# Reordering the filling of a one-core Hyena and gated-MLP pipeline, with a one-sum inverse transform in three of sixteen halves

## The chip, the cores and the metric

One core of one Trainium2 chip runs the whole kernel in one launch. The metric is device microseconds of that core.

## The reference

The input x is 8 sequences of 512 positions by 512 channels. Two layers follow each other, each with a residual and a layer norm behind it:

```python
x = layernorm(x + attn(x)); x = layernorm(x + ffn(x))
# attn (a Hyena operator):
u = x @ in_proj_w.T + in_proj_b                  # 3 * 512 columns
uc = causal_conv1d_3taps(u, short_w) + short_b   # per channel
x0, x1, v = split(uc)
k = filter_network(sin, sin, sin) * decay        # 512 channels by 512 positions
v = irfft(rfft(v * x1, n=1024) * rfft(k, n=1024) / 1024)[..., :512] + (v * x1) * filter_bias
y = (v * x0) @ out_proj_w.T + out_proj_b
# ffn: int codes below 64, zero point 128, one scale for each row
y = (silu(x @ Wg.T) * (x @ Wu.T)) @ Wd.T         # 1408 hidden columns
```

## The kernel before, in words

**Tiling.** TensorE works in blocks of 128. A sequence has 4 position blocks and its channels are split into two *halves* of 256, so there are 16 halves. The MLP works on *pairs* of position blocks (256 positions); there are 16 pairs too. fp32 operands are split into a high and a low part and multiplied with three terms (`three`, L825 on).

**The pipeline.** `program()` writes one list of steps, and every engine walks the same list, taking the kinds it has a branch for. The list runs over n = 0 to 19 and eleven beats each. In iteration n: half n is projected (`ip`), convolved with three taps (`conv`), multiplied (`v1`: v*x1) and transposed (`tv`, `vsplit`); half n-1 gets its four block spectra (`fw`, two in beat 0, one in beats 3 and 6), the ten products spectrum x filter (`mul` on VectorE, two parts each, and `acc` on GpSimd, which adds them from a ring of four `tmp` slots into `acc`), the split of each finished block (`psplit`: ScalarE high part, GpSimd low part) and the inverse transform (`iv`), followed by the multiplication with X0 (`y`) and its split (`z`); pair n-2 gets its output projection (`op`), residual (`resid`, `ln1`) and LN1 (`stat`, `var`, `norm`); pair n-3 is transposed (`x2t`, `x2split`) and goes through the MLP (`gu`, `silu`, `hmul`, `hhi`, `hlo`, `dn`), one of eleven hidden blocks in each beat; pair n-4 is scaled (`ln2`), added (`x2add`), normalized and stored. So n = 0 to 2 are the *filling*, with no MLP, and n = 17 to 19 the *draining*.

**Products of a block.** Block i of a half is the sum over j <= i of spectrum j times filter i-j; `PAIRS_OF_BEAT` puts (0,0) in beat 0, (0,1) and (0,2) in beat 1, and so on to (3,3) in beat 8. `LIGHT` are the halves 0, 1 and 15. There the additions of block 3 are VectorE's *own* (L745 to L750), from `x2` slots or, for half 15, from `cv`; GpSimd skips them (L605).

**The inverse.** For each of two channel groups and two parts, `acc_hi` times the high and low inverse matrix side by side (256 columns), and `acc_lo` times the high one (128 columns): 8 matmuls, and a bank with two sums. `y` on VectorE takes three operations: low sum x X0, high sum x X0, their addition.

**Banks.** `bank` is a ring of two PSUM banks for ip, tv, iv, op, xt and x2t; until the MLP begins the two `gate_up` banks widen it to four. `free_bank` waits for the reading of the use before. The spectra have two banks of their own; a spectrum waits for the last product of the spectrum two before it.

**The network.** Three layers: a matmul (`net`, TensorE, L849), six operations on VectorE (same step name, L672 to L682), a sine on ScalarE (`sin`, L489); then `kmm` (L855) makes the filter from the last sine, and `spec` (L864, L866) its eight spectra, evicted by ScalarE (L493). The weights come as 18 floats stages (`stage`: ScalarE high part, GpSimd low part) and 35 integer code tiles (`code`: ScalarE; the down weights are saved to memory again by SP), through a few slots.

**The sequence of DMAs** is SP's: it walks the same list (`code`, `xload`, `resid`, `wdload`, `store`) and waits in order.

Lines that the prediction names: L741 product, L747, L749 and L750 own additions, L611, L617, L618 additions on GpSimd, L622 low part of a block, L639 bias into the residual rows, L648 rstd, L697 low part of x, L760 to L764 y, L778 scaling of `down`, L643 its addition, L558 normalization, L831 to L833 the three terms, L923 and L924 inverse, L945 transposition of x2, L962 and L963 gate and up, L973 and L974 down.

Of the kernel before, what the change touches and what calls it, by code (L numbers as in the profile page):

```python
# [177 lines left out]
def program():  # L178
    steps = [("xt", 0, 0), ("xt", 0, 1), ("xsplit", 0, 0), ("xsplit", 0, 1), ("stage", 0), ("stage", 1), ("xt", 0, 2),
             ("xt", 0, 3), ("xsplit", 0, 2), ("xsplit", 0, 3), ("net", 0), ("bias", )]  # L180
# [11 lines left out]
def build(nc, x, win, wout, wg, wu, wd, fwd, shifted, inv, decay, z_pos, w0, w1, w2, w3, net_cols, fbias,  # L192
          conv_w, conv_cols, gate_cols, up_cols, down_row, out_row, identity, out):
    ctx = ExitStack()
    with ctx:
# [271 lines left out]
        def _(act):  # L467
# [13 lines left out]
            for kind, *at in steps:  # L481
# [51 lines left out]
                elif kind == "psplit":  # L533
                    n, i = at
                    last = ("mul", n, i, i, 1)
                    if last in own:
                        act.wait_ge(own_added, own[last] + 1)
                    else:
                        act.wait_ge(temp_added, temp[last] + 1)
# [498 lines left out]
```

## Time and profile before

| | us |
|---|---|
| median of 3 runs | 1102.07 (1100.32 to 1104.34) |
| profiled execution | 1102.69, of which span 1100.9 |
| TensorE busy | 1036.5 (94%), weight loads 837.8 (76%) |
| VectorE, ScalarE, GpSimd busy | 803.1 (73%), 466.2 (42%), 625.9 (57%) |
| mean granted clock of TensorE | 0.970 |

The share of the span is an average over the stages: TensorE is at 90% or more in all slices from about 150 to 960 us of the span and at 70 to 90% before. The chain that ended last is 70% TensorE, 15% VectorE, 5% ScalarE, 4% GpSimd. In the rows below a time at the start of a line is microseconds from the start of the span; brackets give the idle time of the engine before the instruction and what ended it.

### The profile page before, as it was taken

How to read it: one execution, taken by the hardware profiler on the slowest of the kernel's cores; microseconds unless marked ns; L12 is line 12 of the kernel's file. 1: busy time of each engine (PE TensorE's matmuls, PEld its weight loads, DVE VectorE, ACT ScalarE, POOL GpSimd, SP SyncE). 2: the span in 40 equal slices, each digit the busy share in tenths (PEclk: the TensorE clock that was granted, in tenths of full speed). 3: DMA queues.
4: the chain of work that ended last, by engine and by line, in shares of the span. 5: the costliest groups of instructions: out<-in, count | busy, mean ns of one | idle time of the engine just before them, and what ended most of it. 6: DMA issues, size and time to landing. Idle time of an engine off the chain costs nothing.

```text
span 1100.9 us, 18043 instructions
## 1 busy us (share of the span) xinstructions
PE 1036.5 (94%) x6378; PEld 837.8 (76%) x6378; DVE 803.1 (73%) x1470; ACT 466.2 (42%) x995; POOL 625.9 (57%) x662
## 2 busy tenths in 40 slices
PE   7887869999999999999999999999999999979996
PEld 4465658888888888788888888888888888867774
DVE  5667777786877778786777778787777878777443
ACT  4554343444434444443444344443445344424242
POOL 4554636475674756576674766576574667572211
PEclk9897879999999999999999999999999999989998
DMA  7543311212123212212122211312121212222232
GB/s 226 169 150 120 101 58 58 82 45 88 48 77 95 79 59 67 97 49 86 49 78 87 87 52 65 99 56 80 55 78 49 87 49 63 72 58 77 87 94 79
DMA packets 51639, 89.53 MB, mean 81 GB/s; under 512 B 6298, under 2 KB 11034, under 8 KB 51550
## 3 DMA queue, kind: packets, MB, share of 16 engines
q1 hardware_dynamic: 50786, 88.12, 25.7%
q8 instruction: 51, 0.84, 0.3%
q10 hardware_dynamic: 764, 0.27, 0.1%
q14 instruction: 38, 0.31, 0.1%
HBM read 77.09 MB, written 11.27 MB: 80 GB/s over the span
## 4 chain that ended last, share of the span: by engine, by line
PE 70%; DVE 15%; issue 5%; ACT 5%; POOL 4%; DMA 1%; ACTq 1%; POOLq 0%; DVEq 0%
PE gate_up L962 10%; PE gate_up L963 10%; PE bank L831 9%; PE bank L833 8%; PE bank L832 8%; PE down L973 6%; PE down L974 6%; PE bank L923 2%; DVE hid_lo L821 2%; PE bank L945 2%; DVE tmp L741 1%; PE spectrum L831 1%; PE spectrum L833 1%; DVE hid L815 1%; PE spectrum L832 1%
## 5 line engine op out<-in xcount | busy, mean ns | idle before, releaser
L580 ACT ACTIVATE hid<-gate_up,gate_scale 128x256 f32<-128x256 f32 x176 | 83.0, 472 | 223.0 <-PE gate_up L963 221.8
L962 PE MATMUL gate_up<-x2T_hi,wg_sb 128*128 128x256 f16 x704 | 165.9, 276 | 0.0
L963 PE MATMUL gate_up<-x2T_lo,wg_sb 128*128 128x256 f16 x704 | 164.0, 273 | 0.0
L962 PE MATMUL gate_up<-x2T_hi,wu_sb 128*128 128x256 f16 x704 | 163.9, 273 | 0.0
L963 PE MATMUL gate_up<-x2T_lo,wu_sb 128*128 128x256 f16 x704 | 163.8, 273 | 0.0
L617 POOL TENSOR_TENSOR acc<-acc,tmp 128x256 f32<-128x256 f32 x148 | 114.9, 776 | 81.4 <-DVE tmp L741 72.0
L741 DVE TENSOR_TENSOR tmp<-spectrum,filt 128x512 f32<-128x512 f32 x235 | 159.5, 681 | 0.0
L973 PE MATMUL down<-wd_sb,hid_hi 128*128 128x512 f32 x352 | 148.3, 421 | 11.7 <-DVE tmp L778 7.2
L831 PE MATMUL bank<-xT_hi,win_hi 128*128 128x512 f32 x360 | 150.2, 417 | 1.2 <-POOL win_lo L598 0.6
L833 PE MATMUL bank<-xT_hi,win_lo 128*128 128x512 f32 x360 | 144.5, 401 | 0.0
L832 PE MATMUL bank<-xT_lo,win_hi 128*128 128x512 f32 x360 | 144.1, 400 | 0.0
L815 DVE SCALAR_TENSOR_TENSOR hid<-gate_up,up_scale,hid 128x256 f32<-128x256 f32 x176 | 84.2, 479 | 78.6 <-ACT hid L580 78.5
L974 PE MATMUL down<-wd_sb,hid_lo 128*128 128x512 f32 x352 | 139.4, 396 | 0.0
L587 ACT ACTIVATE hid_hi<-hid 128x256 fp32r<-128x256 f32 x176 | 73.5, 418 | 132.0 <-DVE hid L815 132.0
L821 DVE TENSOR_TENSOR hid_lo<-hid,hid_hi 128x256 fp32r<-128x256 f32 x176 | 111.3, 632 | 24.2 <-ACT hid_hi L587 24.2
L622 POOL TENSOR_TENSOR acc_lo<-acc,acc_hi 128x512 fp32r<-128x512 f32 x64 | 81.9, 1280 | 80.7 <-ACT acc_hi L542 80.7
L611 POOL TENSOR_TENSOR acc<-acc,tmp 128x512 f32<-128x512 f32 x87 | 114.5, 1316 | 6.2 <-DVE tmp L741 6.2
L706 DVE SCALAR_TENSOR_TENSOR cx<-bank,taps,cx 128x511 f32<-128x511 f32 x62 | 46.4, 748 | 95.0 <-ACT cx L523 95.0
L523 ACT ACTIVATE cx<-bank,conv_bias,taps 128x1 f32<-128x1 f32 x186 | 77.9, 488 | 77.7 <-PE bank L833 77.7
L962 PEld LDWEIGHTS gate_up<-x2T_hi,wg_sb 128*128 128x128 bf16 x704 | 68.7, 98 | 53.8 <-issue 47.3
L618 POOL TENSOR_TENSOR acc<-acc,tmp 128x256 f32<-128x256 f32 x148 | 108.3, 732 | 0.0
L973 PEld LDWEIGHTS down<-wd_sb,hid_hi 128*128 128x128 f32 x352 | 66.4, 189 | 24.0 <-issue 7.8
(170 smaller groups left out, 2258.6 us busy)
## 6 DMA issues: line engine op xcount, KB each, us to landing
wd_sb<-wd_scratch SPq DMA_DIRECT2D x176, 256.0 KB, 2.6
xstage<-in_x SPq DMA_DIRECT2D x32, 256.0 KB, 4.2
x<-in_x SPq DMA_DIRECT2D x28, 256.0 KB, 2.8
out<-x SPq DMA_DIRECT2D x28, 256.0 KB, 3.2
x<-in_win SPq DMA_DIRECT2D x12, 256.0 KB, 5.1
acc<-in_decay SPq DMA_DIRECT2D x4, 256.0 KB
x<-in_wout SPq DMA_DIRECT2D x4, 256.0 KB, 2.6
x2T_hi<-in_wu SPq DMA_DIRECT2D x4, 256.0 KB, 3.7
```

The lines of the kernel that those rows point to most:

```text
L611: G.tensor_tensor(acc[:, i, :, :], acc[:, i, :, :], temp_of(first), ALU.add).then_inc(temp_added, 1)
L617: G.tensor_tensor(acc[:, i, 0, :], acc[:, i, 0, :], t[:, 1, :], ALU.subtract)
L618: G.tensor_tensor(acc[:, i, 1, :], acc[:, i, 1, :], t[:, 0, :], ALU.add).then_inc(temp_added, 1)
L741: TT(dst, spectrum[j % 2][:, :, :], k_part, ALU.mult).then_inc(made_done, 1)
L821: TT(hid_lo[:, k % 2, :], hid[:, k % 2, :], f32(hid_hi[:, k % 2, :]), ALU.subtract).then_inc(h_lo_done, 1)
L831: mm(out_ap, ah, bh, start=k == 0, stop=False)
L832: mm(out_ap, ah, bl, start=False, stop=False)
L833: last = mm(out_ap, al, bh, start=False, stop=k == n - 1)
L962: mm(dst, w[:, kb, rows(q)], x2T_hi[:, kb, ts], start=kb == 0, stop=False)
L963: last = mm(dst, w[:, kb, rows(q)], x2T_lo[:, kb, ts], start=False, stop=kb == CB - 1)
L973: mm(down[b][:, :], hid_hi[:, k % 2, rows(b)], wd_sb[:, k % 3, :], start=q == 0, stop=False)
L974: last = mm(down[b][:, :], hid_lo[:, k % 2, rows(b)], wd_sb[:, k % 3, :], start=False, stop=q == HB - 1)
```

## The change

1. *Network chain.* VectorE's six operations become a step `arg` of their own. `arg` 2 stands at the end of beat 2, where `net` 2 stays at the end of beat 3 on TensorE; `sin` 2 moves from beat 4 to 3, `kmm` from 5 to 4, and the first three pairs of `spec` from beats 7, 8, 9 to 6, 7, 8.
2. *Beat 6.* While there is no MLP work (n = 1, 2) the shared products (`op`, `ip`) stand before the spectrum; with MLP work the order stays.
3. *x transposed in one beat.* At n = 1 all four transpositions of sequence 1 stand in beat 9 instead of 9 and 10.
4. *Beat 0.* The first of the two spectra stands before the transposition of x2, in all n.
5. *One-sum inverse in the light halves.* 12 matmuls of 128 columns into one sum, and `y` in one operation.
6. *Own additions.* Only for halves 0 and 1, and there only for products (0,3) and (1,3). (2,3), (3,3) and all of half 15 go to GpSimd through the `tmp` ring.
7. *Draining.* For n > 16 the scaling and addition of block 1 stand right behind those of block 0. For the last pair the first block's scaling waits only for its own `down` matmuls (`half_down`), VectorE does the additions, and normalizes block 1 while ScalarE normalizes block 0.

```diff
@@ shared, beat_steps, setup_steps, program
+    if n == 1 and beat == 9:
+        steps += [("xt", 1, tb) for tb in range(TB)]
-    if beat in (9, 10) and n > 0 and n % 2 == 1 and n + 1 < HALVES:
+    if beat in (9, 10) and n > 1 and n % 2 == 1 and n + 1 < HALVES:
...
-    steps += spectra + downs + shared(n, beat) if beat == 6 else shared(n, beat) + spectra
+    if beat == 6 and u:
+        steps += spectra + downs + shared(n, beat)
+    elif beat == 0:
+        steps += spectra[:1] + shared(n, beat) + spectra[1:]
+    else:
+        steps += shared(n, beat) + spectra
...
+    if beat == 3 and done and n > HALVES:
+        steps += [("ln2", n - 4, 1), ("x2add", n - 4, 1)]
...
-    if beat == 3 and done:
+    if beat == 3 and done and n <= HALVES:
         steps += [("ln2", n - 4, 1), ("x2add", n - 4, 1)]
...
-SPEC_OF_BEAT = {(0, 7): 0, (0, 8): 1, (0, 9): 2, (1, 0): 3}
+SPEC_OF_BEAT = {(0, 6): 0, (0, 7): 1, (0, 8): 2, (1, 0): 3}
...
-        steps += {1: [("sin", 0), ("net", 1)], 2: [("sin", 1)], 3: [("net", 2)], 4: [("sin", 2)],
-                  5: [("kmm", d) for d in range(TB)]}.get(beat, [])
+        steps += {1: [("sin", 0), ("net", 1), ("arg", 1)], 2: [("sin", 1), ("arg", 2)], 3: [("net", 2), ("sin", 2)],
+                  4: [("kmm", d) for d in range(TB)]}.get(beat, [])
@@ build
-        own = count([s for s in steps if s[0] == "mul" and s[1] in LIGHT and s[3] == TB - 1 and (s[2] or s[4])],
-                    "mul")
+        own = count([s for s in steps if s[0] == "mul" and s[1] < 2 and s[2] < 2 and s[3] == TB - 1 and (s[2] or s[4])], "mul")
@@ vector: y
+                    if ("y", n, i) not in two_sums:
+                        TT(y, sums[:, :, 0, :], y, ALU.mult).then_inc(bank_read, 1)
+                        continue
@@ vector: last pair
+                    if (m, b) == (LAST, 0):
+                        dve.wait_ge(half_down, 1)
...
+                elif kind == "x2add" and at[0] == LAST:
+                    m, b = at
+                    dve.wait_ge(made_done, made["ln2", m, b] + 1)
+                    TT(row_tile(m, b), row_tile(m, b), flat(temp_of(("ln2", m, b))), ALU.add).then_inc(tail_added, 1)
...
+                    if (w, m) == (LN2, LAST):
+                        dve.wait_ge(ln_shift[w], m + 1)
+                        TS(row_tile(m, 1), row_tile(m, 1), rstd[:, w, 1:2], shift[:, w, 1:2], ALU.mult, ALU.add)\
+                            .then_inc(tail_normed, 1)
@@ tensor: iv
+                        if n in LIGHT:
+                            last = three(high, [(acc_hi[:, i % 2, r, rows(c)], acc_lo[:, i % 2, r, rows(c)],
+                                                 inv_parts[:, r, 0, :], inv_parts[:, r, 1, :]) for r in range(2)])
+                            continue
```

## Rows read from the trace of the kernel before

**Rows 1.** Windows: stretch, us, busy us of each engine (instructions), PEclk, DMA share, GB/s.

```profile
60.00:103.40 43.40, 31.16 (x147) 25.61 (x145) 32.43 (x55) 23.22 (x49) 21.06 (x22) 0.84 0.35 111
103.40:152.70 49.30, 34.09 (x148) 28.09 (x148) 37.41 (x65) 18.51 (x43) 26.81 (x28) 0.78 0.40 127
130.00:132.00 2.00, 2.00 (x7) 1.61 (x7) 1.90 (x5) 0.00 (x0) 0.00 (x0) 0.50 0.01 4
276.20:339.50 63.30, 62.72 (x406) 51.58 (x404) 49.00 (x91) 28.16 (x61) 39.43 (x42) 1.00 0.22 66
```

**Rows 2.** Waits of TensorE: total us, times, longest.

```profile
PE bank L945 <- ACT x L558: 10.2, 1, 10.2
PE down L973 <- DVE tmp L778: 7.2, 3, 3.6
```

**Rows 3.** Groups by line; for two lines the durations in ns min/median/max.

```profile
L611 POOL TENSOR_TENSOR acc<-acc,tmp 128x512 f32<-128x512 f32 x87 | 114.5, 1316 | 6.2 <-DVE tmp L741 6.2
L618 POOL TENSOR_TENSOR acc<-acc,tmp 128x256 f32<-128x256 f32 x148 | 108.3, 732 | 0.0
...
L747 DVE TENSOR_TENSOR acc<-acc,x x6: 691/693/921, 79.9 to 146.0; 128x512 f32<-128x512 f32 x6
...
L764 DVE TENSOR_TENSOR cx<-cx,y_low x64: 424/425/1462, 70.5 to 1018.7; 128x256 f32<-128x256 f32 x64
```

**Rows 4.** Timeline of n = 0: start, us, instruction, [idle before <- releaser].

```profile
24.33 1.07 PE L849 MATMUL down<-tmp,hid 64*64 64x512 f32 x2 [0.50 <-ACT tmp L489]
...
27.95 0.79 DVE L672 TENSOR_SCALAR tmp<-down,net 64x512 f32<-64x512 f32 x1
...
34.67 2.68 PE L855 MATMUL down<-out_bias,tmp 64*128 64x512 f32 x4 [3.48 <-ACT tmp L489]
```

**Rows 5.** Timeline, weight loads of one inverse and the next.

```profile
107.79 0.19 PEld L924 LDWEIGHTS bank<-inv_parts,acc_lo 128*128 128x128 f32 x1
...
108.60 0.19 PEld L831 LDWEIGHTS bank<-xT_hi,win_hi 128*128 128x128 f32 x1
```

**Rows 6.** Timeline of n = 1 and the start of n = 2.

```profile
81.50 0.55 PE L831 MATMUL spectrum<-vT_hi,fwd_hi 128*128 128x256 f32 x1 [2.84 <-DVE x L741]
...
86.41 1.30 POOL L611 TENSOR_TENSOR acc<-acc,tmp 128x512 f32<-128x512 f32 x1
...
97.41 1.26 POOL L622 TENSOR_TENSOR acc_lo<-acc,acc_hi 128x512 fp32r<-128x512 f32 x1 [6.13 <-ACT acc_hi L542]
...
103.37 0.47 PE L831 MATMUL gate_up<-xT_hi,win_hi 128*128 128x512 f32 x1 [1.99 <-DVE xT_lo L697]
```

**Rows 7.** Timeline of n = 2.

```profile
113.30 3.01 POOL L639 TENSOR_TENSOR x<-x,out_bias 128x512 f32<-128x512 f32 x2 [2.57 <-DMA x<-in_x]
...
124.78 0.55 PE L923 MATMUL gate_up<-inv_parts,acc_hi 128*128 128x256 f32 x1 [3.07 <-POOL acc_lo L622]
...
149.23 0.70 POOL L648 TENSOR_TENSOR rstd<-var_eps,minus_half 128x2 f32<-128x2 f32 x1 [8.02 <-DVE var_eps L792]
```

**Rows 8.** Timeline, beat 0 of n = 4 and of n = 5.

```profile
215.09 1.25 PE L945 MATMUL bank<-ident,x 128*128 128x128 f32 x8 [0.45 <-DVE xT_lo L697]
216.10 0.36 PE L831 MATMUL spectrum<-vT_hi,fwd_hi 128*128 128x256 f32 x1
...
276.12 1.04 PE L945 MATMUL bank<-ident,x 128*128 128x128 f32 x8
276.92 0.36 PE L831 MATMUL spectrum<-vT_hi,fwd_hi 128*128 128x256 f32 x1
```

**Rows 9.** Timeline of n = 16, beat 3.

```profile
975.55 0.68 DVE L778 TENSOR_TENSOR tmp<-down,down_scale 128x512 f32<-128x512 f32 x1
...
976.38 0.76 PE L973 MATMUL down<-wd_sb,hid_hi 128*128 128x512 f32 x1 [3.62 <-DVE tmp L778]
```

**Rows 10.** Timeline of the tail.

```profile
1091.41 1.29 DVE L778 TENSOR_TENSOR tmp<-down,down_scale 128x512 f32<-128x512 f32 x2 [1.29 <-PE down L974]
...
1097.66 1.04 SPq L451 DMA_DIRECT2D out<-xstage  x2
```

More of the change, by code:

```diff
@@ L134, in beat_steps @@
         steps += [("mul", *p, 0), ("acc", *p, 0), ("mul", *p, 1), ("acc", *p, 1)]
-    if beat != 6:
+    if beat != 6 or not u:
         steps += downs
@@ L138, in beat_steps @@
         steps += [("wdload", *u)]
-    if beat == 4 and done:
+    if beat == 4 and done and n - 4 < LAST or beat == 3 and n - 4 == LAST:
         steps += [("stat", LN2, n - 4, 0), ("stat", LN2, n - 4, 1), ("var", LN2, n - 4)]
@@ L179, in program @@
     steps = [("xt", 0, 0), ("xt", 0, 1), ("xsplit", 0, 0), ("xsplit", 0, 1), ("stage", 0), ("stage", 1), ("xt", 0, 2),
[L180 removed]
+             ("xt", 0, 3), ("xsplit", 0, 2), ("xsplit", 0, 3), ("net", 0), ("arg", 0), ("bias", )]
     for n in range(HALVES + 4):
@@ L205, in build @@
         made = count(steps, "mul", "ln2")
-        own = count([s for s in steps if s[0] == "mul" and s[1] in LIGHT and s[3] == TB - 1 and (s[2] or s[4])],
-                    "mul")
-        own_early = sum(s[1] < 2 for s in own)
+        own = count([s for s in steps if s[0] == "mul" and s[1] < 2 and s[2] < 2 and s[3] == TB - 1 and (s[2] or s[4])], "mul")
+        two_sums = count([s for s in steps if s[0] == "y" and s[1] not in LIGHT], "y")
         temp = {s: k for k, s in enumerate(s for s in steps if s[0] == "ln2" or s[0] == "mul" and (s[2] or s[4])
@@ L354, in temp_of @@
             if step in own:
-                home = x2[:, 2 + own[step] % 2, :] if step[1] < 2 else cv[:, own[step] % 2, :]
-                return home.rearrange("p (r c) -> p r c", r=2)
+                return x2[:, 2 + own[step] % 2, :].rearrange("p (r c) -> p r c", r=2)
             return tmp[:, temp[step] % 4, :, :]
@@ L457, in _ @@
                     elif m == 1:
-                        sp.wait_ge(own_added, own_early)
+                        sp.wait_ge(own_added, len(own))
                     else:
@@ L534, in _ @@
                     n, i = at
[L535 to L539, printed above, removed]
+                    act.wait_ge(temp_added, temp["mul", n, i, i, 1] + 1)
                     if 4 * n + i >= 2:
@@ L556, in _ @@
                     act.wait_ge(ln_shift[w], m + 1)
-                    for b in range(2):
+                    for b in range(1 if (w, m) == (LN2, LAST) else 2):
                         A(row_tile(m, b), row_tile(m, b), ACT.Identity, scale=rstd[:, w, b:b + 1],
@@ L639, in _ @@
                     G.tensor_tensor(row_tile(m, b), row_tile(m, b), out_bias[:, :], ALU.add).then_inc(res_biased, 1)
-                elif kind == "x2add":
+                elif kind == "x2add" and at[0] < LAST:
                     m, b = at
@@ L974, in _ @@
                         last = mm(down[b][:, :], hid_lo[:, k % 2, rows(b)], wd_sb[:, k % 3, :], start=False, stop=q == HB - 1)
+                        if (m, q, b) == (LAST, HB - 1, 0):
+                            last.then_inc(half_down, 1)
                     last.then_inc(down_done, 1)
```

29 lines of the change are left out of this document (21 added, 8 removed).

## The prediction

> **What bounds the kernel now.** I read busy time by stretch first. In a settled half, 276.2 to 339.5, TensorE is busy 62.72 of 63.30 us at granted clock 1.00, VectorE 49.00 and GpSimd 39.43: TensorE's instructions are the bound, and an edit there counts only if it takes TensorE time or a TensorE wait away. In the two stretches of the filling, 60 to 103.4 and 103.4 to 152.7, TensorE is busy 31.16 and 34.09 at clocks 0.84 and 0.78, VectorE 32.43 and 37.41, GpSimd 21.06 and 26.81. No engine is full; a chain through all four sets the pace, and TensorE runs at its 1.2 GHz level for part of it (130 to 132: busy all 2.00 at clock 0.50) [rows 1]. The waits of TensorE say where that chain ends: 10.2 us in one piece for the first LN1 rows of pair 0, up to the first transposition of x2 at 152.75, and 7.2 us in three pieces for L778, the scaling of `down` [rows 2]. Then the timelines of those places.
>
> **The change part by part** (times of the profiled execution: 1102.69 us, span 1100.9; 0.6 above the median 1102.07).
>
> *A, network chain, n = 0.* Layer 2's six steps on VectorE began at 27.95, behind two convolutions, though TensorE had made their input by about 25.4 (two matmuls, 1.07 from 24.33). They now start there: 2.5 earlier. `kmm`, which waited 3.48 until 34.67 for their sine [rows 4], can start at 32. But one projection (12 matmuls, about 3 us) that ran before it, under the chain, now stands behind it, so TensorE idles from 28.3 to 32 just as long and has 3 us more to do after. 2.7 earlier, 3 more work: 0. Bounds -1 (less contention in the chain) and +2.5 (that projection at half clock). The stages 9 and 10 now queue on ScalarE behind the sine, 5 us later; they are first needed by the projections after 60, so nothing.
>
> *The prices in a light half.* The inverse: 12 instead of 8 matmuls, each with its own weight load. From the load at 107.79 to that at 108.60 are seven steps, 0.116 each, although every other matmul is only 128 wide [rows 5]: loads set the pace. Four more cost 0.45 us per inverse at full clock (bounds: 0, if the narrow matmuls hide, and 0.9 at half clock). The multiplication by X0 loses two of three VectorE operations, 0.42 each and up to 1.46 for the one with both inputs in SBUF: 0.9 less [rows 3]. So each inverse-to-z link gets 0.45 shorter. The products (2,3) and (3,3) go from VectorE (0.69 for the first addition, two halves of it for the second) to GpSimd at 1.32 + 2 x 0.73 = 2.8 each [rows 3].
>
> The isolated matmul gap that the Trainium skill gives ("TensorE: Matmul & The Clock Gate", Back-to-back issue gap) is 56 ns at 128 columns, by which the new inverse would be 0.67 and so cheaper; its own section on LDWEIGHTS (columns / 1.2, 107 ns) is what the rows show. By the first the sum would be 3 us lower at most.
>
> *B, n = 1 (60 to 103.4).* In beat 6 the fourth spectrum stood before the last projection and waited 2.84 for a product until 81.50; half clock followed [rows 6]. With the projection first there is no pause: it ends near 81 instead of 87.6, and its eviction, now behind z on ScalarE, is 3.8 earlier. VectorE has also dropped two y operations and the own additions. Product (2,2) on GpSimd, 86.41 before, begins about 2.3 earlier and ends at 87.0. From there GpSimd's own queue rules: split 0.6 on ScalarE and 1.3, products (2,3) and (3,3) 2 x 2.8, so the last split is at 94.5, not 96.7. The 6.13 us that GpSimd idled there [rows 6] cover the moved additions. Behind it on ScalarE: split and z 0.95, four halves of x at 0.5, then one VectorE copy 0.6: projections of n = 2 start at 98.5 rather than 103.37: -4.9. All four transpositions of x in one beat keep ScalarE from putting codes between them (1.0, contained in this).
>
> *C, n = 2 (103.4 to 152.7).* The residual rows reach GpSimd at 113.30 by DMA [rows 7]; the transfers are queued on SP behind the saving and loading of codes, so they gain about 3.3, to 110. Then on GpSimd: two bias additions 2.6, z 0.7, v*x1 1.3, z 0.7, product (1,1) 2.8, split 0.6 + 1.3: inverse 1 at 120.3, not 124.78 (-4.5) [rows 7], after a pause of some 2.6 where it was 3.07. From there: product (1,2) 2.8 and v*x1 1.3 on GpSimd, VectorE's own additions, y and z of block 1 at 128, product (2,2) to 131. The projection of beat 6 no longer waits for the spectrum, whose wait disappears. Last on GpSimd: (2,3) and (3,3), about 136 to 141.6, then rstd 0.7, which ran at 149.23 before [rows 7], and the normalization 0.8: rows at 142.7 if TensorE falls to half clock after the pause as it did, 140.4 if it doesn't. The old pause of 3.07 is the nearest row, so 142.7: -10.0 for B and C together. Bounds -14 and -4 (every GpSimd step that is now behind another one adds its contention).
>
> *D, spectrum leads beat 0.* At n = 3 the first spectrum runs in the shadow of that wait; half clock makes it 1.3: -1.3. At each even n from 4 to 14 the transposition of x2 waits for a bank that xT_lo reads: 0.45, and 1.01 from its start to the spectrum (215.09 to 216.10), where an odd n has no wait and 0.80 (276.12 to 276.92) [rows 8]. A spectrum (six loads at 0.116, 0.7 [rows 5]) ahead of it covers both: 0.66 x 6 = -4.0. In exchange x2's split ends 0.7 later at odd n; its reader is the gate matmul two beats (some 11 us) on. Bounds -4.5, 0.
>
> *E, n = 16.* VectorE scales `down` at 975.55; TensorE waits 3.62 for it, to 976.38, and then runs at half clock [rows 9] for 5 us. VectorE arrives earlier by the two y operations and the two additions (0.9 + 0.7) and TensorE comes 0.45 later by the longer inverse: the wait is 3.62 - 1.6 - 0.45 = 1.6, and I take it that the clock then stays up (2.4 of the 5). 2.0 + 2.4, and 0.1 to 1 later on, where hid_lo stood behind the own additions: -4.5, the longer inverses contained. Bounds -6, and -1 (GpSimd, now with 7 more operations' work, holds the split and with it silu).
>
> *F, n = 17 and 18.* The scaling of block 1 stood behind hmul. The two shorter pieces of [rows 2] are (7.2 - 3.6)/2 = 1.8; with the two scalings adjacent about 0.45 stays: -2.7. hmul waits for silu longer than the scaling takes (0.6), so nothing is late for it.
>
> *G, tail.* Scaling began at 1091.41, behind all four matmuls; the first of two stores was issued at 1097.66 [rows 10]. The first half's matmuls end 0.47 earlier; then on VectorE 0.7 + 0.7 + 0.6 + 0.7 and two statistics 1.2, 0.4 before the old end of statistics; the two normalizations run side by side, the second 0.7 earlier: -0.8. Bounds -1.3, 0.
>
> *H.* The inverses of block 3 of halves 1 and 15 lie where TensorE is full: 2 x 0.45 = +0.9.
>
> Sum: 0 - 10.0 - 1.3 - 4.0 - 4.5 - 2.7 - 0.8 + 0.9 = -22.4: 1080.3 for the profiled execution, 1080 for the median.
>
> **The rivals.** *GpSimd takes over the filling (0.20).* Per light half it gets 5.6 us more, and an operation of it and one of VectorE with two SBUF inputs seem to hold each other up (0.42 against 1.46 [rows 3]). For it: rstd stands behind (3,3) in its queue. Against: its idle 6.13 and 8.02 [rows 6, 7]. If B and C bring 2 instead of 10: 1088.
> The Trainium skill speaks for this one: "SBUF — State Buffer", Who interferes with whom, says that a VectorE instruction with two SBUF inputs and a GpSimd instruction that reads SBUF exclude each other for their whole length. The 1.46 agrees; but the change also takes such operations off VectorE, so the rule cuts both ways.
>
> *The filling is shorter still (0.15).* The clock stays at its upper level after the 2.6 pause, and SP gives the residual rows earlier: B and C -15, 1075.
>
> *Codes are late (0.04).* All 35 codes must be there before x2's split; SP loads them in turn. B and C would be cut to 5: 1085.
>
> *Slower: half clock through the filling (0.05).* The clock fell after a pause of 3 us or less; if the many small pauses now hold it at 0.50 from 60 on, TensorE's work alone is 31.16 x 0.84 / 0.5 = 52 and 34.09 x 0.78 / 0.5 = 53 instead of 43.4 and 49.3, and the last chain to the rows, 8, comes on top: +21. Less the 12.4 of D to H: +9, 1110. It decides once the filling gets more than 12.4 longer. Against: pauses become fewer.
>
> *Nothing moves (0.03)*: what is won is lost to waits in n = 3 and 16: 1101.
>
> **The numbers.** Forecast 0.53, its own range 1075 to 1086. Range for 8 in 10: 1072 to 1091, taking in the shorter filling and GpSimd. Faster by over 0.3% (about what can be told from no change here): 0.92; within 0.3%: 0.03; slower: 0.05.
>
> **What would show it.** First transposition of x2 at 141 to 144 and a spectrum ahead of it (B, C, D); first projection of n = 2 at 98 to 99 (B); `kmm` at 32 (A); no 0.45 wait at even n (D); the wait on L778 at n = 16 under 2 us and clock 1.00 behind it (E); two waits of 0.5 (F); 12 loads at 0.116 in a light inverse. Wrong if the x2 transposition comes after 149, or if TensorE's clock over 60 to 140 is below 0.7.

## The result, and the profile after

| | before | after |
|---|---|---|
| median, us | 1103.2 (1100.32 to 1106.75, 4 runs) | 1078.99 (1076.37 to 1080.01, 4 runs) |
| profiled execution, of which span | 1102.69, 1100.9 | 1076.37, 1074.6 |
| TensorE, VectorE, GpSimd busy | 1036.5, 803.1, 625.9 | 1030.4, 780.8, 640.9 |
| mean granted clock | 0.970 | 0.984 |

The ratio is 0.9776 (95%: 0.9759 to 0.9793): 24 us faster, where 22 were forecast. Windows of the changed kernel that answer to [rows 1] (the two stretches of the filling, a piece of n = 2 at half clock, a settled half):

```profile
56.60:96.00 39.40, 29.71 (x158) 25.25 (x157) 26.67 (x44) 22.13 (x48) 27.06 (x30) 0.91 0.40 123
96.00:137.80 41.80, 33.16 (x170) 27.75 (x171) 29.30 (x51) 19.53 (x44) 30.80 (x33) 0.93 0.48 158
118.50:121.50 3.00, 3.00 (x10) 2.52 (x10) 2.93 (x5) 0.87 (x2) 2.94 (x3) 0.50 0.28 87
259.70:322.40 62.70, 62.57 (x407) 51.71 (x406) 48.37 (x90) 27.74 (x60) 39.40 (x42) 1.00 0.21 65
```

The filling is shorter by 4.0 and 7.6 us, VectorE has lost 6 and 8 us of work in it, GpSimd has gained 6 and 4, and the clock is 0.91 and 0.93. Waits of TensorE from 100 us on, to be set against [rows 2]; then the timeline lines that answer to [rows 4] and [rows 6 to 10]:

```profile
PE bank L980 <- ACT x L571: 4.9, 1, 4.9
PE gate_up L862 <- POOL acc_lo L639: 3.7, 1, 3.7
PE down L1008 <- DVE tmp L799: 3.1, 3, 1.9
```

```profile
24.88 0.80 DVE L689 TENSOR_SCALAR tmp<-down,net 64x512 f32<-64x512 f32 x1 [0.38 <-PE down L880]
...
30.18 1.98 PE L886 MATMUL down<-out_bias,tmp 64*128 64x512 f32 x4 [2.34 <-ACT tmp L503]
...
81.32 1.26 POOL L628 TENSOR_TENSOR acc<-acc,tmp 128x512 f32<-128x512 f32 x1
...
92.64 1.27 POOL L639 TENSOR_TENSOR acc_lo<-acc,acc_hi 128x512 fp32r<-128x512 f32 x1 [0.74 <-ACT acc_hi L552]
...
107.18 2.55 POOL L656 TENSOR_TENSOR x<-x,out_bias 128x512 f32<-128x512 f32 x2 [3.77 <-DMA x<-in_x]
...
117.32 0.30 PE L862 MATMUL gate_up<-inv_parts,acc_hi 128*128 128x128 f32 x1 [3.69 <-POOL acc_lo L639]
...
135.93 0.71 POOL L665 TENSOR_TENSOR rstd<-var_eps,minus_half 128x2 f32<-128x2 f32 x1
...
137.83 1.94 PE L980 MATMUL bank<-ident,x 128*128 128x128 f32 x8 [4.87 <-ACT x L571]
...
198.84 1.15 PE L980 MATMUL bank<-ident,x 128*128 128x128 f32 x8
...
954.66 0.76 PE L1008 MATMUL down<-wd_sb,hid_hi 128*128 128x512 f32 x1 [1.89 <-DVE tmp L799]
955.23 0.63 PE L1009 MATMUL down<-wd_sb,hid_lo 128*128 128x512 f32 x1
...
1065.18 0.69 DVE L799 TENSOR_TENSOR tmp<-down,down_scale 128x512 f32<-128x512 f32 x1 [0.82 <-PE down L1009]
```

Read them from the top. `kmm` starts at 30.18, not 34.67; GpSimd's product (2,2) at 81.32, not 86.41 (3.4 of the 5.1 were gained before the first projection of n = 1, at 56.58 instead of 59.98), and the idle 6.13 ahead of its low part of a block is now 0.74; the residual rows come at 107.18; `rstd`, which had waited 8.02, stands without a wait behind the product (3,3); x2's transposition at n = 4 has no wait and is led by a spectrum. At n = 16 the wait is 1.89 instead of 3.62, but the next matmul takes 0.63: the clock fell all the same. The light inverse loads its weights at a steady pace. From the second of its 12 loads to the first load of the product behind it, the first two and the last two:

```profile
62.58 0.19 PEld L863 LDWEIGHTS gate_up<-inv_parts,acc_hi 128*128 128x128 f32 x1
62.69 0.19 PEld L864 LDWEIGHTS gate_up<-inv_parts,acc_lo 128*128 128x128 f32 x1
...
63.69 0.19 PEld L864 LDWEIGHTS gate_up<-inv_parts,acc_lo 128*128 128x128 f32 x1
63.80 0.19 PEld L862 LDWEIGHTS gate_up<-xT_hi,win_hi 128*128 128x128 f32 x1
```

That is 0.111 a step, (63.80 - 62.58)/11, where [rows 5] had led to 0.116: the loads set the pace, not the 128 columns.

### The profile page after: what moved, and what is told of

It is laid out like the page before. It is cut to its first block, busy times and chain, and to the rows that moved or that the text cites. A ratio compares the mean times of both kernels' runs of the same rounds, so it can differ in the third digit from the quotient of the medians.

```text
span 1074.6 us, 18114 instructions
## 1 busy us (share of the span) xinstructions
PE 1030.4 (96%) x6426; PEld 837.3 (78%) x6426; DVE 780.8 (73%) x1426; ACT 465.0 (43%) x994; POOL 640.9 (60%) x683
## 4 chain that ended last, share of the span: by engine, by line
PE 73%; DVE 9%; POOL 7%; issue 7%; ACT 3%; DMA 1%; ACTq 0%; POOLq 0%; DVEq 0%
PE gate_up L997 11%; PE gate_up L998 11%; PE bank L862 9%; PE bank L864 9%; PE bank L863 9%; PE down L1008 6%; PE down L1009 6%; PE bank L958 3%; POOL acc L628 2%; DVE tmp L756 1%; PE bank L980 1%; POOL acc L635 1%; PE spectrum L863 1%; PE spectrum L864 1%; PE spectrum L862 1%
## 5 line engine op out<-in xcount | busy, mean ns | idle before, releaser
L756 DVE TENSOR_TENSOR tmp<-spectrum,filt 128x512 f32<-128x512 f32 x250 | 169.2, 680 | 0.0
L634 POOL TENSOR_TENSOR acc<-acc,tmp 128x256 f32<-128x256 f32 x156 | 121.0, 776 | 73.9 <-DVE tmp L756 63.9
L852 DVE TENSOR_TENSOR hid_lo<-hid,hid_hi 128x256 fp32r<-128x256 f32 x176 | 114.3, 650 | 25.1 <-ACT hid_hi L600 25.1
L628 POOL TENSOR_TENSOR acc<-acc,tmp 128x512 f32<-128x512 f32 x94 | 123.2, 1310 | 7.2 <-DVE tmp L756 6.9
L635 POOL TENSOR_TENSOR acc<-acc,tmp 128x256 f32<-128x256 f32 x156 | 114.2, 732 | 0.0
L862 PEld LDWEIGHTS bank<-xT_hi,win_hi 128*128 128x128 f32 x360 | 69.2, 192 | 20.9 <-DVE xT_lo L714 3.3
```

What stands on the lines that cost most here:

```text
L628: G.tensor_tensor(acc[:, i, :, :], acc[:, i, :, :], temp_of(first), ALU.add).then_inc(temp_added, 1)
L634: G.tensor_tensor(acc[:, i, 0, :], acc[:, i, 0, :], t[:, 1, :], ALU.subtract)
L635: G.tensor_tensor(acc[:, i, 1, :], acc[:, i, 1, :], t[:, 0, :], ALU.add).then_inc(temp_added, 1)
L756: TT(dst, spectrum[j % 2][:, :, :], k_part, ALU.mult).then_inc(made_done, 1)
L852: TT(hid_lo[:, k % 2, :], hid[:, k % 2, :], f32(hid_hi[:, k % 2, :]), ALU.subtract).then_inc(h_lo_done, 1)
L862: mm(out_ap, ah, bh, start=k == 0, stop=False)
```

## The experiments

Twelve kernels ran, each timed four or five times beside the kernel before, with one of the executions profiled. One of them is the changed kernel once more, and most share whole segments with it, so the scatter of a single profile can be seen. The segments below are read from the timelines: up to the first projection of n = 1 (M1), from there to that of n = 2 (M2), to x2's transposition at n = 3 (M3), n = 16 (M4), n = 17 (M5), n = 18 (M6) and the end of the span. Beside the four groups in which the kernels were timed the kernel before had medians of 1101.8 (the u kernels but u_beat0), 1102.6 (again, u_beat0 and the v kernels), 1104.2 (the w kernels but the last) and 1103.2 (w_x2add); so across groups the ratios are the better measure.

| kernel | median | ratio to before (95%) | M1 | M1-M2 | M2-M3 | M3-M4 | M4-M5 | M5-M6 | M6-end |
|---|---|---|---|---|---|---|---|---|---|
| before | 1103.2 | 1 | 59.98 | 43.39 | 49.38 | 806.11 | 53.20 | 39.83 | 49.01 |
| after | 1078.99 | 0.9776 (0.9759-0.9793) | 56.58 | 39.44 | 41.82 | 801.03 | 49.37 | 39.07 | 47.27 |
| again | 1079.53 | 0.9785 (0.9765-0.9804) | 59.20 | 39.46 | 41.85 | 800.30 | 49.45 | 39.07 | 47.29 |
| v_ln2_16 | 1079.63 | 0.9784 (0.9766-0.9801) | 57.49 | 39.44 | 43.28 | 801.08 | 49.63 | 39.07 | 47.29 |
| u_net | 1079.82 | 0.9805 (0.9785-0.9825) | 58.50 | 39.42 | 42.02 | 801.60 | 49.35 | 39.08 | 47.29 |
| u_beat6 | 1083.94 | 0.9834 (0.9815-0.9854) | 58.17 | 39.46 | 47.57 | 801.74 | 49.35 | 39.07 | 47.28 |
| u_inv | 1084.58 | 0.9850 (0.9831-0.9869) | 56.92 | 41.19 | 44.91 | 801.14 | 51.25 | 38.65 | 47.27 |
| u_own | 1081.17 | 0.9817 (0.9796-0.9838) | 58.57 | 38.15 | 47.32 | 802.22 | 49.38 | 39.07 | 47.28 |
| u_beat0 | 1083.67 | 0.9820 (0.9803-0.9838) | 58.35 | 39.44 | 42.19 | 805.72 | 49.37 | 39.07 | 47.28 |
| v_warm | 1074.92 | 0.9740 (0.9723-0.9757) | 53.62 | 39.44 | 42.64 | 802.26 | 49.43 | 39.06 | 47.26 |
| w_net | 1079.17 | 0.9776 (0.9755-0.9797) | 56.37 | 39.49 | 43.83 | 802.74 | 49.54 | 39.07 | 47.31 |
| w_xt_ln2 | 1078.56 | 0.9773 (0.9750-0.9796) | 54.39 | 40.29 | 41.61 | 803.86 | 49.42 | 40.27 | 48.51 |
| w_best | 1076.77 | 0.9761 (0.9740-0.9782) | 53.40 | 39.60 | 45.69 | 800.21 | 51.08 | 39.15 | 47.31 |
| w_x2add | 1074.05 | 0.9736 (0.9720-0.9752) | 54.05 | 39.43 | 44.63 | 801.11 | 48.85 | 39.07 | 47.27 |

Kernels equal in a segment agree within 0.1 from M1 to M2 and within 0.2 behind M4, but elsewhere they differ: M1 by 2.6 us (by 1.0 among the four with ten filler matmuls), M2 to M3 by 2.8, M3 to M4 by 3.7. Some 1.6 of the last stem, in v_warm, w_net and w_xt_ln2, from the half between n = 8 and 9, 62.4 to 62.5 instead of 60.9, where TensorE waits twice for GpSimd (0.93 and 0.44 in v_warm).

**u_net: the chain undone.** 

> The changed kernel with the old order of the network chain (spectra one beat later, layer 2's VectorE steps behind two convolutions, kmm in beat 5); all else as changed. The changed kernel reaches the first projection of n = 1 at 56.58, the kernel before at 59.98. Theory A (the chain itself brings it: the six VectorE steps take 4.6 us instead of 6.0 with GpSimd idle beside them, and the stretch at half clock behind kmm shrinks): that projection comes at 59.5 to 60.2, and the whole is 1079.0 + 3.2 = 1082. Rival 1 (as predicted, the order of the chain is worth nothing; the 3.4 us come from the other edits of the filling): the projection stays at 56.6 and the whole at 1079. Rival 2 (the gain is taken by a later wait: what A gives at 57 is not there any more at x2's first transposition, since GpSimd's queue rules behind it): projection at 60, x2's first transposition still near 137.8, whole 1079 to 1080.

```diff
-SPEC_OF_BEAT = {(0, 6): 0, (0, 7): 1, (0, 8): 2, (1, 0): 3}
+SPEC_OF_BEAT = {(0, 7): 0, (0, 8): 1, (0, 9): 2, (1, 0): 3}
-        steps += {1: [("sin", 0), ("net", 1), ("arg", 1)], 2: [("sin", 1), ("arg", 2)], 3: [("net", 2), ("sin", 2)],
+        steps += {1: [("sin", 0), ("net", 1)], 2: [("sin", 1)], 3: [("net", 2)], 4: [("sin", 2)],
```

M1 came at 58.50, between the two expectations, and the later segments did not take it back, so rival 2 falls. But the ratio can't be told from the changed kernel's. M1 itself scatters, which "again" looks at.

**u_beat6: beat 6 undone.** 

> The changed kernel with the old order of beat 6 in halves 0 to 2 (spectrum ahead of the last projection). Theory B (a spectrum that waits for its product holds up the projection behind it; the pause is filled when the projection leads): TensorE waits 2.5 to 3 us for a product in beat 6 of n = 1 and of n = 2, the projection's eviction comes some 3 us later, the first projection of n = 2 at 98 to 99 instead of 96.0, x2's first transposition 3 to 5 us later than 137.8; whole 1082 to 1084. Rival (GpSimd's queue of products sets the end of each half, and the order on TensorE costs nothing): first projection of n = 2 within 0.5 of 96.0, x2's within 1 of 137.8; whole 1079.

```diff
-    if beat == 6 and u:
+    if beat == 6:
```

```profile
78.87 0.36 PE L862 MATMUL spectrum<-vT_hi,fwd_hi 128*128 128x256 f32 x1 [2.42 <-DVE x L756]
...
125.09 0.55 PE L862 MATMUL spectrum<-vT_hi,fwd_hi 128*128 128x256 f32 x1 [1.15 <-DVE x L756]
```

The timeline shows the wait for the product again, 2.42, and the projection behind it came at 80.09 instead of 74.70. Yet M1 to M2 is 39.46 against 39.44: at n = 1 the order is worth nothing, as the rival said. It is worth 3 to 6 at n = 2 (47.57 against 41.8 to 44.6), as the theory said. For the whole the medians give 4.4 to 5, the ratios 5 to 6.

**u_inv: the two-sum inverse back in the light halves.** 

> The changed kernel with the old inverse (8 matmuls, both sums) and the old three-operation multiplication by X0 in halves 0, 1 and 15. Theory C (a shorter VectorE link in the filling outweighs four more weight loads per inverse): each inverse takes 0.90 instead of 1.28 us on TensorE, each y 0.4 to 1.5 us more on VectorE; x2's first transposition 1.5 to 3 us later; the inverse of block 3 of halves 1 and 15 gives 2 x 0.4 back where TensorE is full; whole 1079 + 2 - 0.8 = 1080. Rival 1 (the one-sum form brings nothing, GpSimd rules): transposition within 0.5 of 137.8 and the whole at 1078.2, 0.8 less. Rival 2 (VectorE is the pace of the filling): transposition 4 us later or more, whole 1082 or more.

```diff
-                        if n in LIGHT:
+                        if False:
-        two_sums = count([s for s in steps if s[0] == "y" and s[1] not in LIGHT], "y")
+        two_sums = count([s for s in steps if s[0] == "y"], "y")
```

It costs 1.75 in the first segment, up to 3 in the second, 1.88 from M4 to M5, and gives 0.42 back from M5 to M6. In all it is 5 by the medians (1084.58 against 1079.5) and 7 to 8 by the ratios: rival 2 by the whole and by x2's first transposition (143.02), more than the theory had. One share stood in neither expectation: the 1.88 at n = 16, where TensorE's wait for the scaling grows from 1.89 to 3.14 and a later one for hid_lo to 2.11. With it the pace of the filling alone, up to 4.8, is not the whole loss.

**u_own: the additions of (2,3) and (3,3) back on VectorE.** 

> The changed kernel with the additions for the products (2,3) and (3,3) of halves 0 and 1 back on VectorE; those of half 15 stay on GpSimd. Theory (GpSimd is the last link of each filling half: three additions of 0.7 to 1.3 more per product there stand ahead of the split and of rstd): x2's first transposition 1 to 3 us earlier than 137.8, whole 1076 to 1078. Rival 1 (VectorE is the last link, and an addition with two SBUF inputs on it is held up by GpSimd beside it, 1.46 instead of 0.42): transposition 1 to 4 us later, whole 1080 to 1083. Rival 2 (the moved additions lie under another chain): within 0.5, 1079.

```diff
-        own = count([s for s in steps if s[0] == "mul" and s[1] < 2 and s[2] < 2 and s[3] == TB - 1 and (s[2] or s[4])], "mul")
+        own = count([s for s in steps if s[0] == "mul" and s[1] < 2 and s[3] == TB - 1 and (s[2] or s[4])], "mul")
```

Groups by line, 60 to 140 us:

```profile
L766 DVE TENSOR_TENSOR acc<-acc,x 128x512 f32<-128x512 f32 x6 | 4.6, 761 | 0.2
L768 DVE TENSOR_TENSOR acc<-acc,x 128x256 f32<-128x256 f32 x8 | 4.5, 562 | 0.3
L769 DVE TENSOR_TENSOR acc<-acc,x 128x256 f32<-128x256 f32 x8 | 3.3, 416 | 0.0
```

At n = 1 the theory holds (38.15, 1.3 faster: GpSimd is the last link), at n = 2 the rival (47.32, 3 to 5.5 slower). There the residual rows come late too: at 108.61 and 110.88, 11.9 and 14.2 behind M2, and for the second GpSimd waits 0.98 more. Two kernels with the additions of the changed kernel have their second row as late (w_net and w_x2add, 14.4 and 14.2) and need 43.8 and 44.6; so 2.7 to 3.5 of the loss are not the rows'. The rows of this pair don't lie in the additions' scratch (`x2` slots 2 and 3, which the next pair's rows take), so whether the additions delay them is not shown.

**again: the changed kernel once more.** 

> The changed kernel as it is, once more, for the scatter of its marks. In the six profiles so far the two kernels with the old network chain reach the first projection of n = 1 at 59.99 and 58.54, the four with the new one at 56.61, 58.14, 56.89 and 58.58, though these four are alike up to there. Theory (TensorE's clock falls at a moment that differs by some 2 us from run to run, beside kmm, and how much of kmm's 8 matmuls stands at half clock decides): mark between 56.5 and 58.7, and the difference to 56.61 is the difference in the start of the stretch at clock 0.50. Rival (the four differ by their edits): 56.6 within 0.2. Whole 1077 to 1081.

```profile
30.00:32.00 2.00, 0.83 (x1) 0.72 0.09 30
32.00:34.00 2.00, 2.00 (x4) 0.50 0.00 0
...
38.00:40.00 2.00, 2.00 (x5) 0.50 0.69 199
40.00:42.00 2.00, 2.00 (x7) 0.72 0.18 68
```

M1 at 59.20: the same code as 56.58. The windows show most of it. The clock is 0.50 from about 30.9 to 41.1; in the first profile of this kernel 32 to 34 still has 0.72 and the stretch ends before 40. `kmm`'s eight matmuls (start 31.17 and 30.18) take 7.1 and 4.5. The other 1.0 was there before: VectorE's chain for layer 2 begins at 25.88 instead of 24.88. The seven profiles of the new chain with its pause have one of two stretches at 0.50: some 6.8 us (after, v_ln2_16, u_inv: M1 at 56.6 to 57.5, mean 57.0) or 10.2 (again, u_beat6, u_own, u_beat0: 58.2 to 59.2, mean 58.6). So the 3.4 us between the two first profiles at M1 hold luck. The means are 57.9 (new chain) and 59.2 (old, two profiles); among stretches of one length the old chain is 1.5 (u_net, 6.8) and 1.4 (before, 10.3) later.

**u_beat0: beat 0 undone.** 

> The changed kernel with beat 0 in the old order (shared work, with x2's transposition, ahead of both spectra). Theory D (a spectrum first hides the bank wait of 0.45 and a slow start at each even n, and at n = 3 stands in the wait for LN1's rows): the lead between x2's transpositions falls by 0.66 at each even n from 4 to 14 and by 0.7 to 1.3 at n = 3; in all 4.6 to 5.3, whole 1079.0 + 5 = 1084. Rival (xT_lo, which the transposition waits for, is only late because TensorE is early: the 0.45 come back as another wait in the same half): 0 to 2, whole 1079 to 1081.

```diff
-    elif beat == 0:
-        steps += spectra[:1] + shared(n, beat) + spectra[1:]
```

```profile
202.37 1.25 PE L978 MATMUL bank<-ident,x 128*128 128x128 f32 x8 [0.46 <-DVE xT_lo L712]
203.38 0.37 PE L860 MATMUL spectrum<-vT_hi,fwd_hi 128*128 128x256 f32 x1
```

The wait of 0.46 is back, and each way from an odd n to the even one behind it is 0.60 to 0.64 longer, that from n = 3 to 4 some 1.0 (62.40 against a mean of 61.4). M3 to M4 is 805.72 where the twelve others with this order have 800.2 to 803.9 (mean 801.6): 4.1 more. In the new order a spectrum (0.7) stands ahead of M4, so the same work is done 4.8 earlier there; but M4 to M5 takes 49.37 with and without it, so that 0.7 is lost again at n = 16, and 4.1 reach the end (the medians of the group differ by 4.1). Theory D, 0.5 short of its range.

**v_ln2_16: the scalings adjacent at n = 16 too.** 

> The changed kernel with the two scalings of down adjacent on VectorE already at n = 16 (in the changed kernel from n = 17 on). At n = 16 TensorE waits 1.89 for L799 and runs at a clock below 1.00 behind it, and h then waits 4.19 for silu. Theory E (VectorE's order at n = 16 is the last link of that wait): the wait falls to 0.5 to 0.9, the clock stays at 1.00, x2's transposition of n = 17 comes 1.5 to 3 us earlier against that of n = 16; whole 1076 to 1077.5. Rival (GpSimd, which holds ScalarE's split and so silu, is the last link): wait 0.5 but hid_lo later by as much, whole within 0.5 of the changed kernel.

```diff
-    if beat == 3 and done and n > HALVES:
+    if beat == 3 and done and n >= HALVES:
```

```profile
956.11 0.47 PE L1008 MATMUL down<-wd_sb,hid_hi 128*128 128x512 f32 x1 [0.92 <-DVE tmp L799]
956.41 0.40 PE L1009 MATMUL down<-wd_sb,hid_lo 128*128 128x512 f32 x1
```

The wait halves and the clock stays up, as theory E wanted, and M4 to M5 is 49.63 instead of 49.4. So neither the wait nor the clock is the last link there, as the rival said.

**v_warm: the pause ahead of `kmm` filled.** 

> The changed kernel with ten matmuls more (128x512, result unused) in the pause of 2.34 us that TensorE makes for the last sine ahead of kmm. Theory (the pause makes the clock fall, and the 7 to 10 us at 0.50 behind it cost 3 to 4 us of the way to the first projection of n = 1): no stretch at 0.50 between 28 and 45, kmm at 30.2 to 30.5, that projection at 53.5 to 54.5 instead of 56.6 to 58.6, whole 1076 to 1077 if nothing later takes it back. Rival (the clock falls whatever fills the pause, or the stretch is hidden under the spectra's evictions on ScalarE): projection within 0.5 of 57.5 and whole at 1079.

```diff
                     if d == 0:
+                        for r in range(10):
+                            mm(filter_banks[3], win_hi[:, r % CB, 0:P], xT_hi[:, r % CB, :], start=True, stop=True)
                         pe.wait_ge(net_sin, 3)
```

```profile
34.00:36.00 2.00, 2.00 (x10) 1.00 0.21 66
36.00:38.00 2.00, 2.00 (x10) 1.00 0.61 183
```

```profile
53.62 0.80 PE L862 MATMUL bank<-xT_hi,win_hi 128*128 128x512 f32 x1
...
953.77 0.47 PE L1010 MATMUL down<-wd_sb,hid_hi 128*128 128x512 f32 x1 [1.89 <-DVE tmp L799]
```

(Windows on TensorE, then its timeline.) The stretch at 0.50 is gone, M1 is 53.62, 4.3 below the mean of the seven, and all of it reaches the end: 1074.92 against 1079.53, with intervals that don't touch. The runs lie within 0.9 us (1074.62 to 1075.55), those of the changed kernel beside them within 3.1; but the three later kernels with the same ten matmuls scatter by 1.7 to 3.7, so the narrow range isn't shown to come from them. At n = 16 this profile has the same wait of 1.89 and no fall of the clock, and M4 to M5 is 49.43 against 49.37 with the fall. Of the nine profiles with a wait of 1.89 to 1.91 there, seven have the fall (after, again, u_net, u_beat6, u_own, u_beat0, w_xt_ln2) and two don't (v_warm, w_net), and all nine need 49.35 to 49.54.

**w_net: the old chain, clock held.** 

> The changed kernel with the old network chain, and with its pause ahead of kmm (3.5 us) filled by 14 matmuls whose result is unused; to be set against the changed kernel with ten such matmuls in its own pause, 1074.9, where the clock stays at 1.00 and the first projection of n = 1 starts at 53.60. Eight profiles of the chain as it is put that mark at 56.6 to 59.2 (new chain, seven kernels, mean 57.9) and at 58.5 and 60.0 (old chain). Theory (without the clock the new chain is worth what the prediction reckoned before rounding it to 0, or less: kmm 4.5 earlier, but 12 matmuls of 0.235 = 2.8 moved behind it): mark at 55.3, 1.7 later; whole 1076.5. Rival (the chain is worth the whole 3.4 of the pair of profiles): mark at 57, whole 1078.

The edits are those of u_net and v_warm, with 14 matmuls. M1 is 56.37, 2.8 behind v_warm, by the theory 1.7, by the rival 3.4: between the two. The medians differ by 4.2, the ratios by 4.0; 1.2 of it stand from M2 to M3, within the scatter there. The chain on VectorE in v_warm and then in w_net, with GpSimd's split of `win` beside it:

```profile
24.50 2.52 POOL L611 TENSOR_TENSOR win_lo<-x,win_hi 128x512 fp32r<-128x512 f32 x2 [3.43 <-ACT win_hi L499]
25.91 1.40 DVE L691 TENSOR_SCALAR tmp<-tmp 64x512 f32<-64x512 f32 x1
27.34 0.42 DVE L693 TENSOR_SCALAR tmp<-tmp 64x512 f32<-64x512 f32 x1
27.79 0.68 DVE L695 SCALAR_TENSOR_TENSOR tmp<-tmp 64x512 f32<-64x512 f32 x1
```

```profile
29.81 2.91 POOL L611 TENSOR_TENSOR win_lo<-x,win_hi 128x512 fp32r<-128x512 f32 x2
...
30.17 1.40 DVE L693 TENSOR_SCALAR tmp<-tmp 64x512 f32<-64x512 f32 x1
31.60 1.66 DVE L695 SCALAR_TENSOR_TENSOR tmp<-tmp 64x512 f32<-64x512 f32 x1
...
42.78 1.98 PE L897 MATMUL down<-acc,cx 128*128 128x512 f32 x4 [0.48 <-DVE acc L708]
```

`kmm` is 4.8 later in the old order (35.15 against 30.37): 3.3 by the later start (28.40 against 25.07 for the first step) and 1.5 by steps that stand beside GpSimd. The 12 matmuls moved take 2.8 of it back, and 0.48 more is a wait for the kernel's sum, which the moved projection hides in the new order.

**w_xt_ln2: x's beat and the scalings at n = 17 and 18 undone, on v_warm.** 

> The changed kernel with the ten matmuls ahead of kmm, and two edits of the change undone that lie 800 us apart and are read at different marks: x's four transpositions of n = 1 again two in beat 9 and two in beat 10, and at n = 17 and 18 the scaling of block 1 again behind hmul. Theory: the first undone makes the first projection of n = 2 1.0 later than 93.04 (ScalarE puts codes between the halves of x), of which x2's first transposition keeps less than 1, since GpSimd's queue is the last link there; the second makes the wait on L799 at n = 17 1.8 longer and at n = 18 as much, x2's transposition of n = 18 1.0 to 1.4 later, the end 2 to 2.7 later. Whole 1074.9 + 2.5 to 3.5 = 1078. Rival (neither is on the path: silu is held up at n = 17 too): marks within 0.3, whole 1075.

M1 to M2 is 0.85 longer, M2 to M3 within the scatter (41.61). M5 to M6 is 1.21 and M6 to the end 1.24 longer, and TensorE's waits on this scaling grow from 3.1 to 5.5. Both as the theory had it. The median, 3.6 above v_warm's, fits the sum of 3.3.

**w_best: pauses of the filling filled, half 15's additions on VectorE.** 

> The changed kernel with the ten matmuls ahead of kmm, and two edits more that lie apart. First: four more pauses of TensorE in the filling get matmuls with unused results, 19 before the inverse (0,2) (pause 5.80), 5 before the first projection of n = 2 (2.18), 12 before the inverse (1,1) (some 4) and 12 before x2's first transposition (4.3), so that no pause is over 2. Theory: the stretches at 0.50 at 80 to 89, 113 to 119 and 134 to 141 go, and x2's first transposition comes 2 to 4 us earlier than 135.69. Rival (VectorE and GpSimd carry the chain, a slow TensorE stands beside them): under 1 us. Second: the additions of half 15's products into block 3 are VectorE's own again, as in the kernel before, since at n = 16 VectorE idles 4.20 while GpSimd's queue (two x2 additions, three products) keeps ScalarE from silu. Theory E2 (GpSimd is the last link at n = 16): from x2's transposition at n = 16 to that at n = 17 47.5 to 48.5 instead of 49.4. Rival (VectorE then scales down later, as in the kernel before): 50 to 51. Whole by the theories 1070 to 1072, by both rivals 1076.

```diff
+KEEP = {("iv", 0, 2): 19, ("ip", 2, V, 0): 5, ("iv", 1, 1): 12, ("x2t", 0, 0): 12}
...
+                if (kind, *at) in KEEP:
+                    keep_busy(KEEP[(kind, *at)])
...
-        own = count([s for s in steps if s[0] == "mul" and s[1] < 2 and s[2] < 2 and s[3] == TB - 1 and (s[2] or s[4])], "mul")
+        own = count([s for s in steps if s[0] == "mul" and (s[1] < 2 and s[2] < 2 or s[1] == LAST) and s[3] == TB - 1
+                     and (s[2] or s[4])], "mul")
```

```profile
93.00 0.47 PE L872 MATMUL gate_up<-xT_hi,win_hi 128*128 128x512 f32 x1 [3.49 <-DVE xT_lo L722]
...
117.09 0.30 PE L872 MATMUL gate_up<-inv_parts,acc_hi 128*128 128x128 f32 x1 [2.16 <-POOL acc_lo L647]
...
955.51 0.77 PE L1027 MATMUL down<-wd_sb,hid_hi 128*128 128x512 f32 x1 [2.71 <-DVE tmp L809]
```

```profile
84.00:88.00 4.00, 3.82 (x34) 1.00 0.49 165
...
116.00:120.00 4.00, 2.91 (x14) 0.69 0.48 132
120.00:124.00 4.00, 4.00 (x11) 0.50 0.01 3
```

(The timeline, then windows on TensorE.) At n = 1 the rival holds. From 83 to 89 us TensorE ran at 1.00 here and at 0.50 in v_warm, and M2 came at 93.00 against 93.06: a slow TensorE stood beside the chain. At n = 2 the question stays open: pauses of 3.49 and 2.16 were left, the clock fell behind both (0.70 from 92 to 96, then as shown), and M2 to M3 is 45.69, longer than in any kernel that keeps the edits of the filling; the residual rows came 13.3 behind M2 (106.27). Whether the added matmuls themselves cost something there isn't separated. The second rival holds: at n = 16 the wait is 2.71 and M4 to M5 is 1.65 longer (51.08 against 49.43).

**w_x2add: the x2 additions of n = 16 on VectorE.** 

> The changed kernel with the ten matmuls ahead of kmm, the two scalings of down adjacent at n = 16 too, and at n = 16 both additions of the scaled down to x2 on VectorE (0.7 each, as in the tail) instead of GpSimd (1.27 each). There VectorE idled 4.20 for silu, which ScalarE could not issue before the split of GpSimd's sum; TensorE waited 1.89 for the scaling. Kernels with the old order there, or with half 15's additions back on VectorE, need 49.6 and 51.1 from x2's transposition at n = 16 to that at n = 17, the changed kernel 49.4 whether its clock fell behind the wait or not. Theory E2 (GpSimd's queue ahead of the split is the last link, and 2.5 us less in it come through): 47.0 to 48.3, whole 1073 to 1074. Rival (what GpSimd gains ends at the next product, which VectorE now makes later): 49.2 to 49.8, whole 1075.

```diff
-                elif kind == "x2add" and at[0] < LAST:
+                elif kind == "x2add" and at[0] < LAST and at[0] != SPARE:
-                elif kind == "x2add" and at[0] == LAST:
+                elif kind == "x2add" and at[0] in (SPARE, LAST):
```

```profile
953.33 0.86 DVE L809 TENSOR_TENSOR x<-x,cv 128x512 f32<-128x512 f32 x1
...
954.94 0.47 PE L1016 MATMUL down<-wd_sb,hid_hi 128*128 128x512 f32 x1 [1.80 <-DVE cv L805]
...
956.20 1.27 POOL L631 TENSOR_TENSOR acc<-acc,tmp 128x512 f32<-128x512 f32 x1 [1.42 <-DVE tmp L759]
```

M4 to M5 is 48.85, 0.5 to 0.6 below the changed kernel and v_warm, 0.8 below v_ln2_16, which has the adjacent scalings too: between the two expectations. GpSimd, relieved of 2.5, then idles 1.42 for a product that VectorE makes later. The median, 1074.05, is the lowest of all, but not told apart from v_warm.

## Why the prediction was right or wrong

The total was right: 22.4 off were forecast, 24.2 came between the medians. Part of that is luck. In the pair of profiles the segments give 3.4 (A), 11.5 (B, C), 5.1 (D with one inverse of H), 3.8 (E) and 2.5 (F, G and the other inverse), together 26.3 where the same terms of the sum are 0, 10.0, 4.85, 4.5 and 3.05. A to C brought 4.9 more, of which some 2 at M1 and 1 at M2 to M3 are scatter of single profiles, E to H 1.2 less, so errors of opposite sign cancel in part. The terms, taken one by one:

- **A (0 forecast).** Mis-sized. "2.7 earlier, 3 more work" put `kmm` at 32; it came at 30.2, and 4.8 earlier than in the old order (w_net). That the six steps stand less beside GpSimd in the new place (4.6 instead of 6.0) was only a bound of the term (-1), and that the projection behind `kmm` hides a wait (0.48) was not in it. It is worth 2.8 with the clock held; as it ran, with the clock falling, 1.3 between the mean marks, and the rest of the pair's 3.4 is scatter.
- **Prices.** The pace of the loads, 0.111, was right. Where it was reckoned against the dropped `y` operations ("each link 0.45 shorter"), it was short: u_inv shows 5 us in all.
- **B (-4.9; measured -3.95).** The size was near, the reason half wrong. "With the projection first there is no pause", and an earlier eviction was to bring the product (2,2) forward: u_beat6 has the pause again and the same M2. Against M1 that product came 1.7 earlier, not 2.3. Undone alone, the one-sum form is worth 1.75 and x in one beat 0.85, and the moved additions cost 1.3; together 1.3 of 3.95. The other 2.6 have no single owner: GpSimd's idle of 6.13 is closed to 0.74, but no run shows which edits do that together.
- **C (B and C -10.0; measured -11.5, and -10.5 with the mean of M2 to M3, 42.9, of the seven kernels equal there).** Rows were forecast at 142.7 and came at 137.8, of which 3.4 stem from M1. GpSimd's order was as written: from the product (1,1) to `rstd` it waits only 2.92 for z and 0.74 for each split. The scatter of 2.8 in the seven equal kernels follows the residual rows: where the second row's addition starts 12.4 to 12.6 behind M2 (after, again, u_net) the segment is 41.8 to 42.0, at 13.1 (v_ln2_16, v_warm) 42.6 to 43.3, at 14.2 to 14.4 (w_net, w_x2add) 43.8 to 44.6. Against kernels with rows as late, beat 6 undone (14.6) costs 2.9 to 3.7, the own additions (14.2) 2.7 to 3.5 and the old inverse (13.1) 1.6 to 2.3. This DMA is GpSimd's longest wait there (3.77), and an earlier issue of it was not tried.
- **D (-5.3; measured -4.8 at M4, -4.1 at the end).** Right, with its 0.66 per even n (0.60 to 0.64). What it had not: the spectrum that leads at n = 16 gains 0.7 ahead of M4 which the next stretch doesn't keep.
- **E (-4.5; measured -3.83).** The wait fell as reckoned, 3.62 to 1.89. The step "I take it that the clock then stays up (2.4 of the 5)" failed twice: it fell in the profile of the changed kernel and in six more with the same wait, and where it stayed up (v_warm, w_net) nothing was won. The 3.8 are the one-sum form (1.88) and half 15's additions on GpSimd (1.65), both read from runs that undo them; 0.3 is left. GpSimd's holding of the split and silu, priced as a risk, is real (VectorE idles 4.2 there), but is worth only 0.6 to 0.8 when relieved.
- **F (-2.7; measured -2.4), G (-0.8; measured -0.5), H (+0.45 each; +0.42 at n = 17).** Right; 0.59 stays at n = 17 where about 0.45 was put. G was not undone by itself: its 0.5 is what F leaves of the last segment.

Of the rivals, "GpSimd takes over the filling" is true as a description (`rstd` stands right behind its last product) and wrong in its price: in u_own the two halves together are slower with the additions on VectorE, though n = 1 alone is 1.3 faster. "The filling is shorter still" wanted the clock to stay up behind a pause of 2.6 ahead of the second inverse of n = 2; the pause was 3.69, and the clock fell (0.50 from 118.5 to 121.5). "Half clock through the filling" didn't come about (0.91 and 0.93), and for n = 1 w_best shows that the clock is not on the chain; for n = 2 no run does.

## What to carry to other kernels

Undo each edit alone and read the marks between which it lies: a total near the forecast hid a term off by 1 to 3 us, a reason that was half wrong, and a clock that costs nothing in one place and 4.6 us in another. See how far the marks of equal code scatter first. Before pricing a stretch at half clock, ask whether TensorE is the last link there: filling the pause paid ahead of `kmm`, where full work follows, and not at n = 1; at n = 16 the time was the same with the fall and without it. When a chain of small VectorE steps is moved, look at what GpSimd does at the new time; the durations change with it.

## What the runs showed of the hardware

- Behind the same pause (2.33 to 2.35) ahead of `kmm`, in seven profiles of the same code up to there, the granted clock fell to 0.50 between 30.0 and 33.2 us and stayed there for 6.8 us (three profiles) or 10.2 (four). A pause of 1.89 to 1.91 at n = 16 was followed by the fall in seven profiles and not in two.
- Ten matmuls with unused results in that pause kept the clock at 1.00 from 20 to 54 us in all four kernels that have them, with M1 at 53.4 to 54.4; 14 did so in the longer pause of w_net.
- A VectorE TENSOR_SCALAR of 64x512 took 0.42 with GpSimd idle and 1.40 beside GpSimd's subtraction, a SCALAR_TENSOR_TENSOR 0.68 and 1.66. The Trainium skill ("SBUF — State Buffer", Who interferes with whom) lists `tensor_scalar` among the instructions that can take the port pair shared with GpSimd, and two SBUF inputs as another way to contend; the trace agrees with both.
- Matmuls of 128x128 fp32 and their weight loads, one for each, start 0.111 us apart at full clock.
